# Cross-attention query products taken out of the tile loop: a stage of their own, four tiles wide, with the products kept in DRAM

## The chip, the cores and the metric

One core of a Trainium2 chip runs the whole kernel. The metric is the device time of one execution in microseconds (us). The engines are TensorE (PE in the profile, with its weight loads as PEld), VectorE (DVE), ScalarE (ACT), GpSimd (POOL) and SyncE (SP), which issues every data DMA. SBUF is the on-chip memory of the engines, PSUM the eight banks into which TensorE writes.

## The reference, cut to what matters

```python
x = x + xattn(layernorm(x), ctx_768)     # x: (64, 32, 512); ctx_768: (64, 257, 384)
x = x + attn(layernorm(x))               # self-attention with a position bias
x = x + ffn(layernorm(x))                # gated, fake-quantized

def xattn(h, c):                         # 16 heads of 64
    q, k, v = h @ Wq, c @ Wk, c @ Wv
    scores = einsum('bhsd,bhkd->bhsk', q, k) / 8
    return (softmax(scores) @ v) @ Wo + bo
```

The change is in `xattn` alone.

## The kernel before

The 2048 tokens (64 batches of 32) are 16 tiles of 128 tokens, so a tile holds four batches. The three layers are three stages, one after the other. In the first, `pe_cross_tile` walks the tiles in a hardware loop. It never forms k or v. For each head it multiplies q by Wk first ("QK", `pe_qk` L468), which gives the query products `qk` with 384 rows, and then by the transposed context ("CT", `pe_ctxT`). The values are formed in the same way: probabilities by context ("PV"), then by Wv ("WV") and by Wo ("WO").

Many products are made in float32 precision out of reduced-precision parts: an operand is split into a high part (ScalarE copies it with rounding, `act_split`) and a low part (VectorE subtracts, `dve_low` L695), and three products high*high, high*low and low*high are added up in PSUM. The scores S, PV and WO are made so. The query projection Q (L464, 128x128 operands) and QK (L475, 64 rows, two heads side by side in the two halves of the array) are plain float32 products, which stand in the profile as two instructions each.

TensorE's order in one tile is written out by hand: for each batch b the scores S(b, 0..3) of four groups of rows; between them the transposes PT and PL of the previous batch's probabilities, then its PV(0..2), and the transposes CT of the next batch's context. Batch 0 has no previous one in the tile: there the transposes XT of the next tile's normalized x and its projection Q(0), Q(1) stand. After batch 3 come QK for the next tile in six parts, with PT, PL and PV of batch 3 between them, then WV, then WO. VectorE, ScalarE and GpSimd have lists in the same order; each bank has three semaphores (filled, copied, drained) that count its uses. GpSimd splits the context rows (`pool_split`, L863 high, L866 low). VectorE's list holds the layernorm of the tile after next (19 small dependent steps and two wide ones), the row maxima (L799), the reciprocals (L774) and scaling of probabilities (L777), all low parts, and `oT` (L791). SyncE's list holds the loads of context (L887), x and the stores of the result.

Of the kernel before, what the change touches and what calls it, by code (L numbers as in the profile page):

```python
# [6 lines left out]
ALU = mybir.AluOpType  # L7
# [29 lines left out]
def cross_units(last):  # L37

    u = []

    def pT(b):
        return [(("PT", b, 0), "t1"), (("PT", b, 1), "t0"), (("PL", b), "t1")]

    def pv(b, m):
        return [(("PV", b, m), ("o0", "o1")[(b * 3 + m + 1) % 2])]

    def qk(i):
        banks = (("s0", "s1"), ("q0", "q1"))[i % 2]
        return [(("QK", i // 3, i % 3, par), banks[par]) for par in range(2)] if not last else []

    def ct(b, c):
        return [(("CT", b + 1, c), ("t0", "t1")[c % 2])] if not (last and b == 3) else []

    def q(n):
        return [(("Q", n), ("q0", "q1")[n])] if not last else []

    for b in range(4):
        before = b > 0
        u.append((("S", b, 0), "s0"))
        u += pT(b - 1)[0:2] if before else []  # L60
        u.append((("S", b, 1), "s1"))
        if not last and b == 0:
            u.append((("XT",), "o0"))
        u.append((("S", b, 2), "s0"))
        u += pT(b - 1)[2:3] if before else []
        u.append((("S", b, 3), "s1"))
        u += pv(b - 1, 0) if before else []
        u += ct(b, 0) + ct(b, 1)
        u += pv(b - 1, 1) if before else q(0)
        u += ct(b, 2)  # L70
        u += pv(b - 1, 2) if before else q(1)
    u += qk(0) + pT(3)[0:2] + qk(1) + pT(3)[2:3] + qk(2) + pv(3, 0) + qk(3) + pv(3, 1) + qk(4) + pv(3, 2) + qk(5)
    u += [(("W", 0), "t0"), (("W", 1), "t1"), (("WO",), "o1")]
    return u
# [61 lines left out]
def build_kernel(nc, x, ctx_768, Wq, Wk, Wv, Wo, bo, a_Wq, a_Wk, a_Wv, a_Wo, rel_emb, clip_x, clip_down,  # L136
# [22 lines left out]
    with ctx:  # L159
# [10 lines left out]

# [6 lines left out]
        x_ln = sb("x_ln", [P, D], F32)  # L177
        x_res = sb("x_res", [P, D], F32)
        x_nrm = sb("x_nrm", [P, D], F32)
# [8 lines left out]
        wq = sb("wq", [P, KD, INNER], F32)  # L188
        qk = sb("qk", [P, 2, 4, KC, 4, P], F32R)
        wkT = sb("wkT", [P, KI, DC], F32)  # L190
        xnT = sb("xnT", [P, KD, P], F32)
        p_last = sb("p_last", [P, 512], F32)
        qT = sb("qT", [P, KI, P], F32)

        aT_low = nc.alloc_sbuf_tensor_at("aT_low", [P, KI, P], F32R, offset=sb.where["xnT"])
        aT_high = nc.alloc_sbuf_tensor_at("aT_high", [P, KI, P], F32R, offset=sb.where["qT"])
# [4 lines left out]
        bo_all = sb("bo_all", [P, D], F32)  # L201
        oT = sb("oT", [P, KC, HEADS, 4, SQ], F32)
        wk_raw = nc.alloc_sbuf_tensor_at("wk_raw", [P, KC, INNER], F32, offset=sb.at - KC * HEADS * P * 4)
        c_raw = sb("c_raw", [P, 2, DC], F32)
        c_nat = [sb(f"c_nat{i}", [P, 2, 2, DC], F32R) for i in range(2)]
        cT = [sb(f"cT{i}", [P, 2, KC, SKP], F32R) for i in range(2)]
        probs = [sb(f"probs{i}", [P, 4, SKP], F32) for i in range(2)]
        pT = sb("pT", [P, 2, 2, 512], F32R)
        c_last = sb("c_last", [P, 2, KC], F32)

        rem_rows = nc.alloc_sbuf_tensor_at("rem_rows", [NB, DC], F32, offset=sb.where["probs0"])
        remT = sb("remT", [P, 2, KC, NB], F32R)
        nmax = sb("nmax", [P, 4], F32)
        den = sb("den", [P, 4], F32)
        rden = sb("rden", [P, 4], F32)

# [75 lines left out]
        s_wq = sem("wq_loaded")  # L292
        s_wvo = sem("wv_wo_bo_loaded")
        s_xln = sem("x_ln_loaded")
        s_xres = sem("x_res_loaded")
# [1411 lines left out]
```

## Time and profile before

| | before |
|---|---|
| median of 3 runs | 1826.18 us (1825.54 to 1827.83) |
| span of the profiled execution | 1826.2 us |
| one tile in the steady loop | 70.05 us |
| last WO of cross-attention begins | 1162.24 us |
| TensorE busy over the span | 95% |

The profile's page gives nothing around the span: the times are those of the span, and the span of the profiled execution stands 0.0 us from the median. How to read it: busy shares of TensorE are of a pipelined engine, so the distance from one group's start to the next group's start says what a group really takes; VectorE and ScalarE times can be taken as they stand.

### The profile page before, as it was taken

The page shows a single profiled execution, that of the slowest core. Times are in us where ns is not written, and L with a number is a line of the kernel's source. Part 1 is how long each engine was busy: PE and PEld are TensorE (multiplying, and loading weights), DVE is VectorE, ACT ScalarE, POOL GpSimd, SP SyncE. Part 2 cuts the span into 40 slices and gives each one's busy share as a digit, 9 for nine tenths or more (in the row PEclk, how much of TensorE's full clock was granted, in tenths as well). Part 3 has the DMA queues.
Part 4 walks back from the last instruction along what each step waited for, and adds up shares of the span by engine and source line. Part 5 has one row for each costly group of instructions (what it writes and reads, how often), then busy time and mean ns, then how long its engine had stood idle before and what let it go on. Part 6 is the DMA issues. An engine that isn't in the chain of part 4 may idle for free.

```text
span 1826.2 us, 41682 instructions
## 1 busy us (share of the span) xinstructions
PE 1732.6 (95%) x15355; PEld 1486.9 (81%) x15367; DVE 1242.4 (68%) x3118; ACT 676.8 (37%) x1471; POOL 309.9 (17%) x183
## 2 busy tenths in 40 slices
PE   6899999999999999999999999899999999996778
PEld 6788988988988988988889888798989898973333
DVE  4767667667677676676676676477868686656686
ACT  3334334334334334334344443322222222213556
POOL 3312212122122122112122121100000000000334
PEclk8999999999999999999999999999999999997899
DMA  5110110110101101001101002501110101003002
GB/s 204 33 35 26 35 43 26 34 39 30 34 29 40 34 29 34 32 30 39 34 26 43 29 26 82 185 29 46 40 57 30 57 29 36 17 23 114 32 16 92
DMA packets 45218, 84.46 MB, mean 46 GB/s; under 512 B 3904, under 2 KB 20352, under 8 KB 45184
## 3 DMA queue, kind: packets, MB, share of 16 engines
q1 hardware_dynamic: 45184, 84.01, 14.0%
q8 instruction: 21, 0.34, 0.1%
q14 instruction: 13, 0.11, 0.0%
HBM read 71.41 MB, written 12.58 MB: 46 GB/s over the span
## 4 chain that ended last, share of the span: by engine, by line
PE 54%; issue 32%; DVE 8%; ACT 4%; POOL 1%; DMA 1%; DVEq 0%; SPq 0%; ACTq 0%; POOLq 0%
PE psum_o L537 15%; PE psum_s L505 10%; PE psum_q L464 6%; PE psum_t L551 5%; PE psum_o L563 5%; PE psum_s L475 3%; PE psum_t L485 3%; PE psum_q L475 2%; PE psum_o L1209 2%; PE psum_s L1209 2%; DVE nmax L799 2%; DVE oT L791 1%; DVE qk L695 1%; PE psum_t L523 1%; ACT probs L652 1%
## 5 line engine op out<-in xcount | busy, mean ns | idle before, releaser
L505 PE MATMUL psum_s<-cT,qk 128*128 128x258 f32 x2304 | 319.1, 289 | 10.7 <-ACT probs L652 7.5
L537 PE MATMUL psum_o<-pT,c_nat 128*128 128x512 f32 x1152 | 312.4, 407 | 0.0
L505 PEld LDWEIGHTS psum_s<-cT,qk 128*128 128x128 f32 x2304 | 292.9, 191 | 23.6 <-ACT probs L652 15.2
L863 POOL TENSOR_TENSOR c_nat<-c_raw,zero 128x768 fp32r<-128x768 f32 x64 | 93.9, 1467 | 870.6 <-PE psum_o L537 521.3
L652 ACT ACTIVATE probs<-psum_s,nmax 128x257 f32<-128x257 f32 x256 | 122.0, 476 | 312.7 <-DVE nmax L799 312.7
L537 PEld LDWEIGHTS psum_o<-pT,c_nat 128*128 128x128 f32 x1152 | 202.5, 188 | 41.4 <-DVE oT L791 0.3
L791 DVE SCALAR_TENSOR_TENSOR oT<-p_last,c_last,psum_o 128x512 f32<-128x512 f32 x192 | 142.8, 744 | 44.2 <-PE psum_o L537 30.6
L799 DVE TENSOR_REDUCE nmax<-psum_s 128x1 f32<-128x257 f32 x256 | 107.3, 419 | 88.6 <-PE psum_s L505 86.4
L695 DVE TENSOR_TENSOR pT<-psum_t,pT 128x512 fp32r<-128x512 f32 x128 | 86.3, 685 | 54.1 <-ACT pT L633 54.1
L464 PE MATMUL psum_q<-xnT,wq 128*128 128x128 f32 x1024 | 123.0, 280 | 0.0
L464 PEld LDWEIGHTS psum_q<-xnT,wq 128*128 128x128 f32 x1024 | 120.5, 197 | 0.0
L866 POOL TENSOR_TENSOR c_nat<-c_raw,c_nat 128x768 fp32r<-128x768 f32 x64 | 119.7, 1870 | 5.0
L931 PEld LDWEIGHTS psum_o<-xnT,w2q 128*128 128x128 f32 x1024 | 118.3, 194 | 2.2 <-issue 1.0
L931 PE MATMUL psum_o<-xnT,w2q 128*128 128x128 f32 x1024 | 118.6, 277 | 0.8 <-issue 0.8
L931 PE MATMUL psum_q<-xnT,w2k 128*128 128x128 f32 x1024 | 117.0, 275 | 0.0
L931 PEld LDWEIGHTS psum_q<-xnT,w2k 128*128 128x128 f32 x1024 | 115.6, 192 | 0.0
L777 DVE TENSOR_SCALAR probs<-probs,rden 128x257 f32<-128x257 f32 x256 | 107.9, 421 | 9.0
L633 ACT ACTIVATE cT<-psum_t 128x256 fp32r<-128x256 f32 x192 | 66.7, 382 | 95.5 <-PE psum_t L485 95.4
L695 DVE TENSOR_TENSOR cT<-psum_t,cT 128x256 fp32r<-128x256 f32 x192 | 75.3, 420 | 34.6 <-ACT cT L633 34.6
L551 PE MATMUL psum_t<-oT,wv 128*64 128x128 f32 x1536 | 87.4, 274 | 1.0 <-DVE oT L791 1.0
L551 PEld LDWEIGHTS psum_t<-oT,wv 128*64 128x64 f32 x1536 | 83.5, 137 | 4.0 <-DVE oT L791 4.0
L1010 PE MATMUL psum_t<-w2o_high,aT 128*128 128x512 f32 x256 | 83.4, 397 | 2.2 <-DVE aT L1112 2.2
(180 smaller groups left out, 2878.1 us busy)
## 6 DMA issues: line engine op xcount, KB each, us to landing
c_raw<-in_ctx_dram SPq DMA_DIRECT2D x64, 384.0 KB, 3.2
out_dram<-x_out SPq DMA_DIRECT2D x32, 256.0 KB, 2.0
x_ln<-in_x_dram SPq DMA_DIRECT2D x16, 256.0 KB, 2.7
x_res<-in_x_dram SPq DMA_DIRECT2D x16, 256.0 KB, 3.2
x_ln<-out_dram SPq DMA_DIRECT2D x16, 256.0 KB, 2.8
x_res<-out_dram SPq DMA_DIRECT2D x16, 256.0 KB, 2.9
x_all<-out_dram SPq DMA_DIRECT2D x1, 4096.0 KB, 15.7
out_dram<-o_sb SPq DMA_DIRECT2D x16, 256.0 KB, 2.0
```

The lines of the kernel that those rows point to most:

```text
L464: i = pe.matmul(ps[:, j * P:(j + 1) * P], wq[:, k, (4 * n + j) * P:(4 * n + j + 1) * P], xnT[:, k, :], start=k == 0, stop=k == KD - 1)
L505: i = pe.matmul(ps[:, 0:SKP], qk[:, part, rg, c, b, :], cT[b % 2][:, moving, c, :], start=n == 0, stop=n == 3 * KC - 1)
L537: i = pe.matmul(ps[:], c_nat[b % 2][:, part, k, cols], pT[:, moving, k, :], start=n == 0, stop=n == 5)
L551: i = pe.matmul(ps[64 * par:64 * par + 64, h4 * P:(h4 + 1) * P], wv[:, c, head * DH:(head + 1) * DH], oT[:, c, slot, :, :], start=c == 0, ...
L652: nc.scalar.activation(probs[b % 2][:, rg, 0:SK], bank[bk][:, 0:SK], ACT.Exp, bias=nmax[:, rg:rg + 1], accum_out=den[:, rg:rg + 1]).then_i ...
L695: nc.vector.tensor_tensor(out, in_(bank[b]), high.bitcast(F32), ALU.subtract).then_inc(drained[b], 1)
L777: nc.vector.tensor_scalar(probs[b % 2][:, rg, 0:SK], probs[b % 2][:, rg, 0:SK], rden[:, rg:rg + 1], None, ALU.mult).then_inc(s_dve, 1)
L791: nc.vector.scalar_tensor_tensor(oT[:, m, :, b, :], p_last[:].rearrange("p (s q) -> p s q", q=SQ), c_last[:, b % 2, m:m + 1], bank[bk][:]. ...
L799: nc.vector.tensor_reduce(nmax[:, rg:rg + 1], bank[bk][:, 0:SK], AX_X, ALU.max, negate=True).then_inc(s_max, 1)
L863: G.tensor_tensor(c_nat[i][:, 0, :, :].rearrange("p k n -> p (k n)"), c_raw[:].rearrange("p k n -> p (k n)"), zero[:].to_broadcast([P, 2 * ...
L866: G.tensor_tensor(c_nat[i][:, 1, :, :], c_raw[:], c_nat[i][:, 0, :, :].bitcast(F32), ALU.subtract).then_inc(s_pool, 1)
L931: i = pe.matmul(ps[:, j * P:(j + 1) * P], w[:, k, (4 * n + j) * P:(4 * n + j + 1) * P], xnT2[:, k, :], start=k == 0, stop=k == KD - 1)
```

## The change

1. A stage before the loop makes Q and QK for all 16 tiles, in four groups s of four tiles. Its operands are split into parts: Wq (`wq`, 2 parts), x (`xnT`), Wk (`wkT`) and q (`qT`); a matmul is now 512 tokens wide. The order in a group is Q(0..3), QK(0..3), Q(4..7), XT of the next group, QK(4..7).
2. QK is copied as whole float32 numbers into `staged`, four slots (j modulo 4), by ScalarE (even heads) and VectorE (odd heads), and stored in `qk_dram`, 3 MiB per tile, 48 MiB in all; each store writes runs of 1536 bytes. A slot is written again only after its store has landed (`wait_slot`).
3. In the loop, one tile's products are loaded back into `raw` (3 MiB), and split in SBUF into `qk`: four high copies of 128x1536 on ScalarE (`act_qk_high`), four subtractions of 128x1536 on VectorE (`dve_qk_low`), both in the loop's batch 3 for the next tile.
4. The loop has no XT, Q, QK and layernorm. Every batch now is the same step: S, PT, PL, PV of the batch before (also across the tile border), CT. WV of the tile before stands in batch 1, WO of it in batch 3; after the last tile a tail does batch 3's PT, PL and PV, then WV and WO.
5. The scaling of probabilities is shared: groups 0 and 1 on ScalarE, 2 and 3 on VectorE. The last key's copies go to ScalarE. Scores use three banks (s0, s1, q0, s0) instead of two. The context has two raw buffers. The split of Wo goes from GpSimd to ScalarE and VectorE, in the first tile; Wv, Wo and x are loaded after the last store of the stage has landed.

```diff
-            for i in range(6):
-                if not last:
-                    pe_qk(pe, t, i // 3, i % 3)
...
+        def pe_group_q(pe, s, j):
...
+            for k in range(KD):
+                for part, moving in PARTS:
+                    m = pe.matmul(ps[:], wq[:, part, k, j * P:(j + 1) * P], xnT[:, moving, k, :, :],
+                                  start=(k, part, moving) == (0, 0, 0), stop=(k, part) == (KD - 1, 1))
...
+        def pe_group_qk(pe, s, j):
...
+            for c in range(KC):
+                places = [empty(pe, project(("QK", s, j, c, par))) for par in range(2)]
+                for part, moving in PARTS:
+                    for par in range(2):
+                        r = slice(64 * par, 64 * par + 64)
+                        m = pe.matmul(places[par][0][:], wkT[r, part, j, c * P:(c + 1) * P], qT[r, moving, j, :, :],
+                                      start=(part, moving) == (0, 0), stop=part == 1)
...
+        def pe_cross_tile(pe, t, section):
+            begun, more = section != "first", section != "last"
             for b in range(4):
+                before = begun or b > 0
+                pe_scores(pe, t, b, 0, section)
+                if before:
+                    pe_probsT(pe, t, b, section)
+                pe_scores(pe, t, b, 1, section)
+                if b == 1 and begun:
+                    pe_wv(pe, t, 0, section)
+                pe_scores(pe, t, b, 2, section)
+                if before:
+                    pe_probs_last(pe, t, b, section)
+                if b == 1 and begun:
+                    pe_wv(pe, t, 1, section)
+                pe_scores(pe, t, b, 3, section)
+                if before:
+                    pe_pv(pe, t, b, 0, section)
+                if more or b < 3:
+                    pe_ctxT(pe, t, b, section, (0, 1))
+                if before:
+                    pe_pv(pe, t, b, 1, section)
+                if b == 3 and begun:
+                    pe_wo(pe, t, section)
+                if more or b < 3:
+                    pe_ctxT(pe, t, b, section, (2,))
+                if before:
+                    pe_pv(pe, t, b, 2, section)
...
+        def act_qk_high(act, t, rg):
+            act.wait_ge(s_qraw, 16 * t + 16)
+            nc.scalar.activation(qk[:, 0, rg, :, :, :].rearrange("p c b (h q) -> p h (c b) q", h=4),
+                                 raw[:, rg, :, :].rearrange("p h (a q) -> p h a q", q=SQ), ACT.Copy).then_inc(s_qhi, 1)
...
+        def dve_cross_tile(dve, t, section):
...
             for b in range(4):
+                before, after = begun or b > 0, more or b < 3
+                qk_next = b == 3 and more
...
+                row_max(b, 3)
+                inverse(b, 2)
+                if qk_next:
+                    dve_qk_low(dve, t + 1, 0, section)
+                if before:
+                    dve_attended(dve, t, b, 0, section)
+                inverse(b, 3)
+                if qk_next:
+                    dve_qk_low(dve, t + 1, 1, section)
+                if after:
+                    ctxT(b, 0)
+                    ctxT(b, 1)
+                norm(b, 2)
                 norm(b, 3)
+                if before:
+                    dve_attended(dve, t, b, 1, section)
+                if b == 3 and begun:
+                    dve_x_out(dve, t, section)
+                if after:
+                    ctxT(b, 2)
+                if qk_next:
+                    dve_qk_low(dve, t + 1, 2, section)
+                if before:
+                    dve_attended(dve, t, b, 2, section)
+                if qk_next:
+                    dve_qk_low(dve, t + 1, 3, section)
...
+        def sp_project_all(sp):
...
+            load_ctx(sp, 0, 0)
+            load_ctx(sp, 0, 1)
+            for s in range(GROUPS):
+                if s < GROUPS - 1:
+                    sp.wait_ge(s_xp, GROUP * (s + 1))
+                    load_x_group(sp, s + 1)
+                if s == 2:
...
+                    load_qk(sp, 0, 0)
+                for j in range(8):
...
+                    for par in range(2):
+                        sp.dma_start(qk_dram[GROUP * s:GROUP * (s + 1), :, 2 * (j // 4) + par, j % 4, :].rearrange("t p n -> p t n"),
+                                     staged[:, j % 4, par, :, :]).then_inc(s_staged[j % 4], 16)
+            for i in range(4):
+                sp.wait_ge(s_staged[i], 64 * GROUPS)
+            sp.dma_start(wv[:], Wv.rearrange("(k p) n -> p k n", p=P)).then_inc(s_wvo, 16)
+            sp.dma_start(wo_raw[:], Wo.rearrange("(k p) n -> p k n", p=P)).then_inc(s_wvo, 16)
```

GpSimd's split for batch b of a tile still waits for the last PV of the batch before (`full(pool, U1(("PV", b - 1, 2), ...))`), and in the loop's batch 0 for the last PV of the tile before.

## Rows read from the trace of the kernel before

**Rows 1.** The page: busy time of each engine, share of the span, instructions.
```profile
PE 1732.6 (95%) x15355; PEld 1486.9 (81%) x15367; DVE 1242.4 (68%) x3118; ACT 676.8 (37%) x1471; POOL 309.9 (17%) x183
```

**Rows 2.** Windows of one loop step: us, busy us per engine (instructions), clock, DMA.
```profile
539.00:609.05 70.05, 69.07 (x573) 60.96 (x572) 47.83 (x124) 28.43 (x73) 14.63 (x9) 1.00 0.11 34
```

**Rows 3.** Timeline of TensorE, one tile: start, us, line, count, idle before it.
```profile
541.15 0.60 PE L449 MATMUL psum_o<-ident,x_nrm 128*128 128x128 f32 x4
541.51 2.40 PE L505 MATMUL psum_s<-cT,qk 128*128 128x258 f32 x18
...
544.18 3.74 PE L464 MATMUL psum_q<-xnT,wq 128*128 128x128 f32 x32
...
547.97 3.74 PE L464 MATMUL psum_q<-xnT,wq 128*128 128x128 f32 x32
...
551.47 1.34 PE L505 MATMUL psum_s<-cT,qk 128*128 128x258 f32 x9
...
552.64 1.04 PE L516 MATMUL psum_t<-ident,probs 128*128 128x128 f32 x8
...
553.44 2.40 PE L505 MATMUL psum_s<-cT,qk 128*128 128x258 f32 x18
...
555.68 0.60 PE L523 MATMUL psum_t<-ident,probs 128*128 128x128 f32 x4
...
557.25 1.56 PE L537 MATMUL psum_o<-pT,c_nat 128*128 128x512 f32 x6
...
558.64 0.60 PE L485 MATMUL psum_t<-ident,c_raw 128*128 128x128 f32 x4
...
562.28 1.24 PE L505 MATMUL psum_s<-cT,qk 128*128 128x258 f32 x9
```

**Rows 4.** The same timeline, the end of the same tile.
```profile
584.55 1.16 PE L475 MATMUL psum_s<-qT,wkT 64*128 64x128 f32 x16
585.64 1.09 PE L516 MATMUL psum_t<-ident,probs 128*128 128x128 f32 x8
...
598.09 5.46 PE L551 MATMUL psum_t<-oT,wv 128*64 128x128 f32 x96
603.48 0.50 PE L563 MATMUL psum_o<-wo_high,aT_high 128*128 128x512 f32 x1
...
609.05 2.31 PE L505 MATMUL psum_s<-cT,qk 128*128 128x258 f32 x18
```

**Rows 5.** Timeline of TensorE at the end of cross-attention.
```profile
1143.37 1.04 PE L516 MATMUL psum_t<-ident,probs 128*128 128x128 f32 x8
...
1162.24 0.39 PE L563 MATMUL psum_o<-wo_high,aT_low 128*128 128x512 f32 x1
```

**Rows 6.** Timeline of the start: the first layernorm on VectorE.
```profile
8.54 0.69 DVE L737 BATCH_NORM_STATS2 stats<-x_ln 128x6 f32<-128x512 f32 x1 [6.56 <-DMA x_ln<-in_x_dram]
...
12.84 0.55 DVE L747 TENSOR_SCALAR x_nrm<-x_ln,lnw 128x512 f32<-128x512 f32 x1
```

**Rows 7.** Groups of instructions by line and shape: busy us, mean ns; idle before.
```profile
L695 DVE TENSOR_TENSOR pT<-psum_t,pT 128x512 fp32r<-128x512 f32 x102 | 68.8, 685 | 43.7 <-ACT pT L633 43.7
L633 ACT ACTIVATE pT<-psum_t 128x512 fp32r<-128x512 f32 x102 | 55.1, 598 | 0.0
L1165 DVE TENSOR_TENSOR w2v_low<-w2v_raw,w2v_high 128x2048 fp32r<-128x2048 f32 x2 | 4.5, 2290 | 1.2 <-ACT w2v_high L1047 1.2
L1320 ACT ACTIVATE h_all<-h_all,tiny 128x1536 f32<-128x1536 f32 x8 | 12.5, 1563 | 0.0
```

**Rows 8.** Windows of stretches with loads of 4 KB rows, then one with stores.
```profile
1144.00:1154.00 10.00, 7.98 (x72) 6.39 (x72) 3.84 (x6) 1.68 (x3) 2.72 (x2) 1.00 1.03 410
...
1822.00:1823.00 1.00, 0.00 (x0) 0.00 (x0) 0.40 (x1) 0.00 (x0) 0.53 (x1) 1.00 0.70 262
```

**Rows 9.** Window around one load of context rows (1536-byte runs).
```profile
567.00:570.00 3.00, 2.78 (x17) 2.42 (x18) 2.50 (x11) 1.80 (x7) 0.00 (x0) 1.00 0.44 131
```

**Rows 10.** Timeline of GpSimd's splits and VectorE beside them.
```profile
503.64 1.47 POOL L863 TENSOR_TENSOR c_nat<-c_raw,zero 128x768 fp32r<-128x768 f32 x1 [7.70 <-PE psum_o L537]
...
504.41 0.72 DVE L713 TENSOR_TENSOR c_last<-remT 128x3 f32 x1
...
541.95 1.99 POOL L866 TENSOR_TENSOR c_nat<-c_raw,c_nat 128x768 fp32r<-128x768 f32 x1
...
543.39 0.70 DVE L777 TENSOR_SCALAR probs<-probs,rden 128x257 f32<-128x257 f32 x1
...
549.20 0.15 DVE L713 TENSOR_TENSOR c_last<-remT 128x3 f32 x1
...
564.15 1.85 POOL L866 TENSOR_TENSOR c_nat<-c_raw,c_nat 128x768 fp32r<-128x768 f32 x1
```

More of the change, by code:

```diff
@@ L539, in pe_pv @@
-            i.then_inc(filled[bk], 1)
-        def pe_wv(pe, t, n, last):
+                    taken(pe, U1(("PT", b, k), t, section))
+                pe.wait_ge(s_nat, 4 * t + b)
+            ps, done = empty(pe, U1(("PV", b, m), t, section))
+            for k in range(2):
+                for part, moving in PARTS:
+                    i = pe.matmul(ps[:], c_nat[(b - 1) % 2][:, part, k, m * P:(m + 1) * P], pT[:, moving, k, :],
+                                  start=(k, part, moving) == (0, 0, 0), stop=(k, part) == (1, 1))
@@ L660, in act_cross_tile, with ctxT @@
+            def ctxT(b, c):
+                act_high(act, U1(("CT", b, c), t, section), cT[(b + 1) % 2][:, 0, c, 0:2 * P], cols(2 * P))
             for b in range(4):
+                before, after = begun or b > 0, more or b < 3
                 exp(b, 0)
-                if b:
-                    act_probsT(act, t, b - 1, last)
+                if before:
+                    for k in range(2):
+                        act_probsT(act, t, b, k, section)
+                if b == 3 and more:
+                    act_qk_high(act, t + 1, 0)
@@ L702, in dve_last_key @@
[L702 to L714 removed]
+                scale(b, 1)
@@ new lines, in act_cross_tile, with act_cross_tail @@
+                act_last_scalars(act, b, 4 * t)
+                if after:
+                    ctxT(b, 2)
+                if b == 3 and more:
+                    act_qk_high(act, t + 1, 2)
+                    act_qk_high(act, t + 1, 3)
+                if section == "first" and b in (1, 2):
+                    act_wo_high(act, b - 1)
+        def act_cross_tail(act):
+            t, section = TILES, "tail"
+            for k in range(2):
+                act_probsT(act, t, 0, k, section)
+            act_probs_last(act, t, 0, section)
+            for n in range(2):
+                act_wv(act, t, n, section)
@@ L874, in pool_cross_tile, with dve_group_stats @@
[L874 to L880 removed]
+        GROUP_STEPS = 22
+        def dve_group_stats(dve, s):
+            ch = Chain(dve, GROUP_STEPS * s, s_lnp)
+            dve.wait_ge(s_xin, 16 * s + 16)
+            for i in range(GROUP):
+                ch.step(nc.vector.bn_stats(group_stats[:, i, :], x_in[:, i, :]))
+            dve.wait_ge(s_lnp, GROUP_STEPS * s + GROUP)
@@ new lines, in sp_cross_tile @@
+        def sp_cross_tile(sp, t, section):
+            begun, more = section != "first", section != "last"
+            for b in range(4):
+                if more or b < 2:
+                    sp.wait_ge(s_nat, 4 * t + (b + 1))
+                    load_ctx(sp, 4 * t, b + 2)
+                if b == 0:
+                    sp.wait_ge(s_qlo, 4 * t + 4)
+                    if more:
+                        load_qk(sp, t, 1)
+                    else:
+                        load_w2(sp, "q")
+            if not more:
+                taken(sp, U1(("S", 3, 3), t, section))
+                for name in "kvo":
+                    load_w2(sp, name)
+            if begun:
+                sp_x1(sp, t, section)
+                sp.dma_start(x_res[:], rows(x_rows, t)).then_inc(s_xres, 16)
```

1064 lines of the change are left out of this document (581 added, 483 removed).

## The prediction

> **What bounds the kernel now.** I began with the page's busy times [rows 1]: TensorE is busy for 95% of the span and the next engine, VectorE, for 68%. A share over the whole span says little about one stage, so I took the windows of one loop step next [rows 2]: of 70.05 us TensorE is busy for 69.07, VectorE for 47.8, ScalarE for 28.4, at full granted clock. The loop is bound by TensorE's own work; its waits are small. What each piece costs is read from the distance between starts in TensorE's timeline [rows 3, 4], since the busy times of overlapping matmuls are too long. The end of the stage is the last WO, 1162.24 + 0.39 = 1162.6 us [rows 5]. What follows (self-attention and FFN, 663.6 us) isn't changed, so the forecast is 663.6 plus the new time of cross-attention.
>
> **What the loop step loses.** Q(0) runs from 544.18 to the last CT at about 547.76 and Q(1) from 547.97 to 551.47, 7.1 us together; XT takes 0.36 [rows 3]. One QK part takes 585.64 - 584.55 = 1.09 us, six take 6.5 [rows 4]. So about 14 us of TensorE per tile go. The loop step that is left, from starts: four S at 1.12 (a pair takes 555.68 - 553.44 = 2.24) is 4.48; PT 0.80; PL about 0.39; three PV at 558.64 - 557.25 = 1.39 are 4.17; CT 0.36 and 0.19 is 0.55: 10.39 us per batch, against 562.28 - 551.47 = 10.81 measured for a batch now [rows 3]. I take 10.39, because the 0.4 of waits is for a score bank (three banks instead of two) and for the low part of CT (which VectorE reaches sooner, having two scalings less ahead of it). With WV 603.48 - 598.09 = 5.39 and WO 609.05 - 603.48 = 5.57 [rows 4], a step is 4 x 10.39 + 10.96 = 52.5 us if nobody waits.
>
> **Do the others keep up?** VectorE loses 12 low parts of QK (12 x 0.685 = 8.2) and gains four of 1536 elements with both inputs in SBUF: nearest row is 2.29 us for 2048 elements, so 4 x 1.75 = 7.0 [rows 7]. The layernorm (12.84 + 0.55 - 8.54 = 4.85 [rows 6]) and half of the scalings (about 3) go too: 47.8 becomes some 37 of 52.5. ScalarE loses 12 x 0.60 and the copies of q, and gains four copies of 1536 at 1.56 [rows 7], eight scalings and eight small copies: about 31 us. Neither is the bound. Loads per step are 3.1 MB more: 8 us of the DMA engines at 400 GB/s [rows 8], hidden under 52 us.
>
> **The tile border.** This is what I expect to cost. In batch 3 ScalarE gets to `qk_high` 2 and 3 only after the third CT, which stands behind WO. Counted from the end of S(3,3): CT(2) ends at 8.8, PV(3,2) at 10.2; ScalarE's `qk_high` 2 and 3 run 9.2 to 12.3; VectorE does `qk_low` 2 from 10.8 to 12.5, attended to 13.3, `qk_low` 3 to 15.0, and only then the first row maximum of the next tile. TensorE would want S(0,3) at 14.9, but it needs the exponential of S(0,0), which shares the bank: 15.0 + 0.4 + 0.5, about 1.1 late. PV(0,0) then waits 1.4 more for the low parts of PT, queued behind on VectorE: 2.5 us per border with no collision. GpSimd's split starts at PV(3,2)'s end, just there. The trace shows such a collision: a three-element addition of two SBUF inputs takes 0.72 and ends with GpSimd's instruction, 0.15 when nothing runs beside it; a scaling takes 0.70; and GpSimd's own low split takes 1.99 beside VectorE, 1.85 otherwise [rows 10]. If each `qk_low` queues with one split of 1.5 to 1.85, `qk_low` 3 ends at 16.9: 4.4 us per border. I take 3.7, nearer to the collision, since both start in the same microsecond. Step: 56.2 us.
>
> On that I weigh the Trainium skill, SBUF — State Buffer, section "Who interferes with whom": a VectorE instruction with two SBUF inputs and a GpSimd instruction that reads SBUF exclude each other for the whole instruction, and the one that comes first has the port. By that page the upper end, 4.4, is the sum for a border, and the time 10 us longer; the row of 1.99 shows far less than a whole instruction lost on GpSimd's side.
>
> **The stage in front.** TensorE per half group (four j): a 512-column matmul in parts takes 5.57/24 = 0.23 us (WO [rows 4]). Q is 12 of them per j, 2.75, four are 11.0. QK is 18 per j in pairs on the two halves of the array. Is a pair as dear as one? Now, 16 instructions of QK take 1.09, 68 ns each, where Q's take 3.5/32 = 110 ns [rows 3, 4]: a pair costs 1.24 of one, not 2. At 512 columns the weight load is a smaller part of each, so I take a pair at 0.24, near one: 9 x 0.24 = 2.15 per j, four are 8.6; at 1.24 they are 10.3, without overlap 16.5. XT is half of 16 transposes, 1. That is 20.6; copies run at 0.60 and 0.69 per bank [rows 7] against 0.7 per pair of banks, so bursts are just covered; I add 0.9 for XT banks and the layernorm steps between: 21.5. DMA per half group: 6.29 MB. Stores run at 262/0.70 = 374 GB/s [rows 8], a load of the same 1536-byte runs at 131/0.44 = 298 with its latency [rows 9]: 16.8 to 21.1 us, plus 1.3 for x. So stores hide, barely, and 21.5 holds. Start: 4 x 0.69 of statistics from 5.2 us, the chain of 3.6 [rows 6], four normalizations, a split of Wq's half (2.3), four low parts: first Q at 19; Q(0..3) 11, Wk's transposes and splits 5, first clock-limited stretch 2: first QK at 37. Stage: 37 + 7 x 21.5 + 9 = 196.5, and 6.5 for the early load of 3.1 MB among the stores and for slot waits: 203 us.
>
> **First tile and tail.** SyncE queues Wv, Wo, bo and x, and behind them the third context load, behind the wait for the last store. Stores end about 12 us after TensorE's last QK, 4.6 MB at 410 GB/s and landing take 14: the third context is there at 27, where TensorE wants it at 17. Tile 0 is 10.5 + 31.2 + 10 + the border, 56 us. Tile 15 has no next products, 52.5. The tail is today's last PT to last WO, 1162.6 - 1143.4 = 19.3 [rows 5].
>
> **Sum.** 203 + 56 + 14 x 56.2 + 52.5 + 19.3 = 1117.6, 45.0 less than 1162.6. The profiled span equals the median within 0.1 us, so 1826.2 - 45 = 1781 us.
>
> **Rivals.**
> 1. *The border costs nothing* (0.12): VectorE's queue recovers within S and PT; a step is 53.0, 14 x 3.2 = 45 less: 1736. For it: VectorE has 15 us free per step. Against it: the order puts two subtractions ahead of the first maximum.
> 2. *Stores are slow* (0.10). Place: `wait_slot`; every store scatters 1536-byte runs over DRAM rows 24 KB apart. At 200 GB/s a half group is 31.5 + 1.3 = 32.8 and the last store ends near 302, the third context comes at 316 instead of 230: +86, 1867, slower. It decides from 241 GB/s down (27.4 us a half group). For it: no row shows such a store in bulk; against it: 374 GB/s for 2 KB runs.
> The Trainium skill, DMA: Bandwidth & Descriptors, "Latency and other measured facts", gives 207 GB/s for a per-partition row pitch of 512 KiB and lets it fall with large powers of two; our pitch isn't a power of two, so the page gives this rival its plausibility and no more. No row here shows a pitch effect.
> 3. *Pairs of QK don't overlap at 512 columns* (0.08): a half group is 29.3, the stage 260, tile 0 waits 6 less: 1832, slower or the same. Against it: 68 ns beside 110.
> 4. *The even step waits in every batch* (0.10): the chain maximum, exponential, PT, high part, low part, PV no longer hides, 0.8 us more per batch, 60 batches: 1829.
> My forecast's own case has 0.60, and 1762 to 1802 as its own range (stage 192 to 215, border 2.5 to 4.4).
>
> **Range and chances.** The high end takes in rivals 3 and 4 in part, the low end part of rival 1: 1746 to 1829. The bound of a measurable change is 0.2%, 3.7 us. Faster: 0.60 + 0.12, half of rival 4 and some of 2 and 3: 0.80. Same 0.05. Slower 0.15, mostly rival 2.
>
> **What the profile will show.** Right: TensorE's start-to-start step near 56 with idle before S(0,3) and PV(0,0) named after VectorE; QK bursts of 8.6 us; DMA share near 0.8 to 1 through the stage; end of stage near 203; a wait for context in tile 0. Wrong: DMA at share 1 with under 300 GB/s and ScalarE or VectorE waiting for `qk_dram` (rival 2), QK of one j near 4.1 (rival 3), idle in each batch (rival 4). What would make me wrong most of all is the multiplier: one microsecond in the step is 15 in the end.

## The result, and the profile after

The changed kernel takes 1852.45 us (median of 4 runs, 1852.04 to 1855.51), against 1826.3 us before in the same session: a ratio of 1.0148, 95% interval 1.0134 to 1.0163. The forecast was 1781 us, with a range up to 1829. The change makes the kernel slower, by 26 us.

The page of the profiled execution (span 1853.7 us), its rows of busy time and of the granted clock; they answer to [rows 1]:

```profile
PE 1693.4 (91%) x13767; PEld 1443.9 (78%) x13767; DVE 1207.7 (65%) x2675; ACT 780.8 (42%) x1699; POOL 315.7 (17%) x179
...
PEclk9998988999999999999999999999999999997899
```

TensorE is busy for 39 us less than before, and the span has grown by some 27 all the same. Where it went is read from windows. First one step of the loop in each of its two forms (the columns of [rows 2], which these rows answer; the first from a tile's first S to the next tile's, the second from WO to WO), then single microseconds inside the first one:

```profile
516.38:574.50 58.12, 55.37 (x409) 49.42 (x408) 37.76 (x79) 29.19 (x79) 15.90 (x9) 0.97 0.26 90
...
627.04:687.50 60.46, 56.77 (x410) 50.27 (x408) 38.06 (x80) 29.33 (x79) 15.89 (x9) 0.94 0.25 87
...
524.00:525.00 1.00, 0.91 (x4) 0.91 (x5) 0.44 (x1) 1.00 (x3) 0.00 (x0) 0.50 1.59 415
525.00:526.00 1.00, 1.00 (x7) 1.00 (x6) 1.00 (x3) 0.40 (x3) 0.00 (x0) 0.50 0.32 98
```

A step was to last 56.2 us. From first WO matmul to first WO matmul thirteen of them last 58.1 to 60.5, on average (1105.38 - 334.46) / 13 = 59.3. Two things show: some 3 us in which TensorE does nothing, and a granted clock under 1.00. The clock is lost in one place, behind the tile border, where it is 0.50 (1.2 GHz) for three microseconds in this step, and for the whole of 644 to 650 in a later one. Over the fourteen borders of this trace behind the first the fall comes 7.4 to 10.1 us behind the tile's first S, and it lasts some 3 us at eight of them and 6 to 7 us at six.

The border in the timeline of TensorE (start, us, line, count, idle before it; it answers to [rows 3]):

```profile
516.38 1.24 PE L583 MATMUL psum_s<-cT,qk 128*128 128x258 f32 x9
517.46 1.03 PE L594 MATMUL psum_t<-ident,probs 128*128 128x128 f32 x8
518.25 1.32 PE L583 MATMUL psum_s<-cT,qk 128*128 128x258 f32 x9
519.93 1.34 PE L583 MATMUL psum_q<-cT,qk 128*128 128x258 f32 x9 [0.36 <-DVE qk L987]
521.11 0.60 PE L601 MATMUL psum_q<-ident,probs 128*128 128x128 f32 x4
524.10 2.30 PE L583 MATMUL psum_s<-cT,qk 128*128 128x258 f32 x9 [2.39 <-ACT probs L796]
526.38 2.06 PE L614 MATMUL psum_o<-pT,c_nat 128*128 128x512 f32 x6
```

The four groups of L583 are S(0,0) to S(0,3). The last begins 7.72 us after the first. In the later step the same two places look like this:

```profile
641.84 1.34 PE L583 MATMUL psum_s<-cT,qk 128*128 128x258 f32 x9 [2.39 <-ACT probs L796]
644.12 2.92 PE L614 MATMUL psum_o<-pT,c_nat 128*128 128x512 f32 x6 [0.94 <-issue]
```

Here S(0,3) still runs at full clock, and a third wait is seen, 0.94 us ahead of PV(0,0); in the first step S(0,3) at half clock covers it.

Back to the first step. S(0,3) waited for ScalarE's exponential of S(0,0), and that for VectorE, whose rows say why (the same stretch, VectorE and GpSimd, answering to [rows 10]):

```profile
516.72 1.47 POOL L1152 TENSOR_TENSOR c_nat<-c_raw,zero 128x768 fp32r<-128x768 f32 x1 [12.58 <-PE psum_o L614]
516.98 2.82 DVE L987 TENSOR_TENSOR qk<-raw,qk 128x1536 fp32r<-128x1536 f32 x1 [0.95 <-ACT qk L730]
...
518.26 3.23 POOL L1155 TENSOR_TENSOR c_nat<-c_raw,c_nat 128x768 fp32r<-128x768 f32 x1
519.72 0.73 DVE L1047 SCALAR_TENSOR_TENSOR oT<-p_last,c_last,psum_o 128x512 f32<-128x512 f32 x1
...
520.38 2.73 DVE L987 TENSOR_TENSOR qk<-raw,qk 128x1536 fp32r<-128x1536 f32 x1
...
523.03 0.41 DVE L1063 TENSOR_REDUCE nmax<-psum_s 128x1 f32<-128x257 f32 x1
```

`qk_low` 2 and 3 (L987) take 2.82 and 2.73 us where the same instruction takes 1.75 alone, and GpSimd's low split 3.23 instead of 1.85 [rows 10]. Each ends about one free duration after the other engine's instruction did: the first at 518.19 + 1.6, the split at 519.80 + 1.7, the second at 521.49 + 1.6. Only then comes the first row maximum, at 523.03.

The stage in front, in the timeline: SyncE ahead of group 1, VectorE and TensorE where that group's x is wanted, then TensorE's second such gap, the first S of the loop, the wait for the third context load in tile 0 and one for the third CT there:

```profile
64.38 11.06 SPq L1209 DMA_DIRECT2D qk_by_tile<-staged  x8
75.49 2.32 SPq L1177 DMA_DIRECT2D x_in<-in_x_dram  x1
...
88.34 2.47 DVE L916 BATCH_NORM_STATS2 group_stats<-x_in 128x6 f32<-128x512 f32 x4 [8.85 <-DMA x_in<-in_x_dram]
...
92.28 1.65 PE L511 MATMUL psum_q<-qT,wkT 64*128 64x512 f32 x6 [9.14 <-DVE staged L966]
...
145.87 1.65 PE L511 MATMUL psum_q<-qT,wkT 64*128 64x512 f32 x6 [9.33 <-DVE staged L966]
...
220.47 0.59 PE L583 MATMUL psum_s<-cT,qk 128*128 128x258 f32 x3 [1.86 <-DVE qk L987]
...
248.13 1.11 PE L554 MATMUL psum_t<-ident,c_raw 128*128 128x128 f32 x4 [8.71 <-DMA c_raw<-in_ctx_dram]
...
278.34 0.69 PE L554 MATMUL psum_t<-ident,c_raw 128*128 128x128 f32 x2 [2.91 <-DVE cT L856]
```

TensorE's row names `staged` L966, VectorE's copies of QK. These were not slow: they stood in VectorE's queue behind `group_stats`, which waited 8.85 us for x. SyncE issued that load only at 75.49, when all sixteen stores of the group before were issued (the row shows the last eight). It takes 12.8 us to land.

Windows in the stage (same columns): a half group without a wait, the half group with the first gap, and a stretch in which the DMA engines do nothing but stores.

```profile
113.80:134.20 20.40, 20.11 (x123) 16.62 (x122) 11.95 (x19) 9.92 (x17) 0.00 (x0) 1.00 0.77 269
...
80.80:113.80 33.00, 23.86 (x137) 19.78 (x136) 18.28 (x44) 11.19 (x20) 0.00 (x0) 0.84 0.70 244
...
44.00:60.00 16.00, 16.00 (x94) 13.24 (x91) 11.25 (x34) 6.75 (x13) 0.00 (x0) 1.00 1.03 365
```

The end of cross-attention, answering to [rows 5], is 1192.39 + 0.39 = 1192.8:

```profile
1192.39 0.39 PE L642 MATMUL psum_q<-wo_high,aT_low 128*128 128x512 f32 x1
```

So this part takes 30.2 us longer than before. What follows it takes 660.9, 2.7 less; no run looks into why.

### The profile page after: what moved, and what is told of

The parts are those of the page before. It is cut to its first block, busy times and chain, and to the rows that moved or that the text cites. A ratio compares the mean times of both kernels' runs of the same rounds, so it can differ in the third digit from the quotient of the medians.

```text
span 1853.7 us, 38185 instructions
## 1 busy us (share of the span) xinstructions
PE 1693.4 (91%) x13767; PEld 1443.9 (78%) x13767; DVE 1207.7 (65%) x2675; ACT 780.8 (42%) x1699; POOL 315.7 (17%) x179
## 4 chain that ended last, share of the span: by engine, by line
PE 53%; issue 31%; DVE 8%; ACT 3%; DMA 3%; SPq 1%; POOL 1%; DVEq 0%; ACTq 0%; POOLq 0%
PE psum_o L614 15%; PE psum_s L583 10%; PE psum_o L629 5%; PE psum_q L642 5%; PE psum_o L495 4%; PE psum_q L583 3%; PE psum_t L554 2%; DVE qk L987 2%; PE psum_t L594 2%; PE psum_o L1545 2%; DMA x_in<-in_x_dram 2%; PE psum_s L1545 2%; ACT qk L730 1%; PE psum_q L511 1%; PE psum_q L601 1%
## 5 line engine op out<-in xcount | busy, mean ns | idle before, releaser
L583 PE MATMUL psum_s<-cT,qk 128*128 128x258 f32 x1728 | 256.7, 294 | 42.4 <-ACT probs L796 38.4
L583 PEld LDWEIGHTS psum_s<-cT,qk 128*128 128x128 f32 x1728 | 229.5, 194 | 55.7 <-ACT probs L796 39.0
L1152 POOL TENSOR_TENSOR c_nat<-c_raw,zero 128x768 fp32r<-128x768 f32 x64 | 94.9, 1483 | 899.2 <-PE psum_o L614 672.3
L796 ACT ACTIVATE probs<-psum_s,nmax 128x257 f32<-128x257 f32 x192 | 91.8, 478 | 250.4 <-DVE nmax L1063 250.3
L987 DVE TENSOR_TENSOR qk<-raw,qk 128x1536 fp32r<-128x1536 f32 x64 | 141.0, 2205 | 15.9 <-ACT qk L730 15.6
L495 PE MATMUL psum_o<-xnT,wq 128*128 128x512 f32 x384 | 93.0, 402 | 4.9 <-DVE xnT L856 2.6
L730 ACT ACTIVATE qk<-raw 128x1536 fp32r<-128x1536 f32 x64 | 93.7, 1493 | 0.0
L495 PEld LDWEIGHTS psum_o<-xnT,wq 128*128 128x128 f32 x384 | 73.6, 194 | 23.4 <-issue 4.4
L629 PE MATMUL psum_o<-oT,wv 128*64 128x128 f32 x1536 | 90.7, 275 | 1.0 <-DVE oT L1047 1.0
L629 PEld LDWEIGHTS psum_o<-oT,wv 128*64 128x64 f32 x1536 | 83.2, 137 | 6.1 <-issue 4.0
L583 PE MATMUL psum_q<-cT,qk 128*128 128x258 f32 x576 | 82.7, 288 | 4.9 <-DVE qk L987 4.9
```

Of the source, the lines that this page charges most:

```text
L495: m = pe.matmul(ps[:], wq[:, part, k, j * P:(j + 1) * P], xnT[:, moving, k, :, :], start=(k, part, moving) == (0, 0, 0), stop=(k, part) == ...
L583: m = pe.matmul(ps[:, 0:SKP], qk[:, part, rg, c, b, :], cT[b % 2][:, moving, c, :], start=(c, part, moving) == (0, 0, 0), stop=(c, part) = ...
L629: i = pe.matmul(ps[64 * par:64 * par + 64, h4 * P:(h4 + 1) * P], wv[:, c, head * DH:(head + 1) * DH], oT[:, c, slot, :, :], start=c == 0, ...
L730: nc.scalar.activation(qk[:, 0, rg, :, :, :].rearrange("p c b (h q) -> p h (c b) q", h=4), raw[:, rg, :, :].rearrange("p h (a q) -> p h a ...
L796: nc.scalar.activation(probs[b % 2][:, rg, 0:SK], bank[bk][:, 0:SK], ACT.Exp, bias=nmax[:, rg:rg + 1], accum_out=den[:, rg:rg + 1]).then_i ...
L987: nc.vector.tensor_tensor(part[1], raw[:, rg, :, :].rearrange("p h (a q) -> p h a q", q=SQ), part[0].bitcast(F32), ALU.subtract).then_inc( ...
```

## The experiments

Every kernel was timed beside the kernel before on one chip (1828.74, 1827.94 and 1827.13 us in the three sessions), and has one profiled execution. "Step" is from first WO matmul to first WO matmul.

| kernel | median us | ratio to before, 95% | step us | clock in a step |
|---|---|---|---|---|
| changed | 1852.45 | 1.0148 (1.0134 to 1.0163) | 58.1 to 60.5 | 0.94 to 0.97 |
| changed, once more | 1854.46 | 1.0153 (1.0140 to 1.0167) | 59.2 to 60.5 | |
| x earlier | 1830.92 | 1.0018 (1.0009 to 1.0028) | 58.1 to 60.5 | |
| split later | 1802.64 | 0.9855 (0.9838 to 0.9871) | 55.7, three of 57.1 to 57.2 | 1.00, in the three 0.97 |
| third CT early, both lists | 1771.66 | 0.9688 (0.9671 to 0.9705) | 53.55 | 1.00 |
| filler behind the wait | 1839.62 | 1.0060 (1.0043 to 1.0077) | 58.63 | 1.00 |
| filler ahead of the wait | 1825.88 | 0.9988 (0.9979 to 0.9997) | 57.59 | 1.00 |
| third context load first | 1858.53 | 1.0158 (1.0142 to 1.0175) | 58.1 to 60.4 | |
| all four edits | 1744.83 | 0.9543 (0.9530 to 0.9556) | 53.55 | 1.00 |
| all but the later split | 1747.17 | 0.9561 (0.9548 to 0.9574) | 53.54 | |
| third CT early, TensorE only | 1802.51 | 0.9865 (0.9849 to 0.9880) | 55.48, the first 57.04 | 1.00, in the first 0.97 |
| VectorE's order only | 1861.58 | 1.0190 (1.0176 to 1.0204) | 58.8 to 61.1 | |

**x half a group earlier.**

```diff
-                if s < GROUPS - 1:
-                    sp.wait_ge(s_xp, GROUP * (s + 1))
-                    load_x_group(sp, s + 1)
+                if s == 0:
+                    sp.wait_ge(s_xp, GROUP)
+                    load_x_group(sp, 1)
...
                 for j in range(8):
+                    if j == 4 and s + 2 < GROUPS:
+                        sp.wait_ge(s_xp, GROUP * (s + 2))
+                        load_x_group(sp, s + 2)
```

> The x rows of group s+2 are loaded in the middle of group s, ahead of four stores, instead of behind the eight stores of group s. Theory A (order of the DMA queue): in the changed kernel VectorE's statistics wait 8.85 and 9 us for x_in, and TensorE stands 9.1 and 9.3 us in groups 1 and 2; both gaps go, the stage ends near 200 instead of 218.5 and the whole is 18 us shorter, about 1834. Rival B (bandwidth of the stores): the stage moves 50 MB at 362 GB/s, the gaps only move to the slots of staged, and the time stays within 5 us of 1852.

Both gaps are gone. The loop's first S, in the timeline of this kernel:

```profile
195.56 0.59 PE L583 MATMUL psum_s<-cT,qk 128*128 128x258 f32 x3 [1.86 <-DVE qk L987]
```

That is 24.9 us earlier: 18.5 of idle time, some 5 of half clock behind it (92.28 to 97.4 and 145.87 to 152.1, from the distances of the starts), and one that I can't place. The span falls by 26.4, the median by 22 (1852.45 to 1830.92). The queue's order is the cause of the stage's loss, shown by mending it.

**GpSimd's split later.** In the loop's batch 0 it waits until S(0,3) is done, when VectorE has both low parts behind it.

```diff
-                pool.wait_ge(filled["o1"], U1.before("o1", t, section))
+                full(pool, U1(("S", 0, 3), t, section))
```

> GpSimd's split of the tile's first batch starts after S(0,3) instead of at the last PV of the tile before; nothing else moves. Theory C (GpSimd and VectorE shut each other out at the border): qk_low 2 and 3 take 1.76 us instead of 2.8 each, S(0,3) waits 0.4 instead of 2.4 us, TensorE's clock stays at 1.00, a step takes 53.5 to 54.5 instead of 59.3, and the whole comes to 1770 to 1785. Rival D (it is the order of VectorE's and ScalarE's lists alone): S(0,3) still waits over 2 us and the time stays within 10 us of 1852.

A window of a step of this kernel:

```profile
500.00:555.67 55.67, 53.75 (x410) 48.15 (x409) 35.77 (x81) 29.06 (x78) 14.49 (x9) 1.00 0.25 94
```

And TensorE's two waits at its border, at S(0,3) and PV(0,0), in the timeline:

```profile
510.22 1.34 PE L583 MATMUL psum_s<-cT,qk 128*128 128x258 f32 x9 [0.98 <-ACT probs L796]
...
512.50 1.66 PE L614 MATMUL psum_o<-pT,c_nat 128*128 128x512 f32 x6 [0.94 <-issue]
```

L987's mean duration falls from 2205 to 1752 ns, and the time by 50 us. That is less than theory C gave and far from D's nothing: the collision is about half of the matter. What is left at the border is the order's part. The clock is back at 1.00 in eleven of the fourteen steps; in the other three it still falls for some 3 us, with the same two waits ahead of it.

**The third CT halfway through WO, on both lists.** TensorE puts CT(3,2) between WO's two halves, so `qk_high` 2 and 3 begin 2.8 us earlier; VectorE takes `qk_low` 2 ahead of `x_out` and `qk_low` 3 ahead of the attended sum.

```diff
             for k in range(KI):
+                if k == KI // 2:
+                    halfway()
...
-                    pe_wo(pe, t, section)
-                if more or b < 3:
+                    if more:
+                        pe_wo(pe, t, section, lambda: pe_ctxT(pe, t, b, section, (2,)))
...
-                if b == 3 and begun:
-                    dve_x_out(dve, t, section)
                 if after:
                     ctxT(b, 2)
                 if qk_next:
                     dve_qk_low(dve, t + 1, 2, section)
-                if before:
-                    dve_attended(dve, t, b, 2, section)
+                if b == 3 and begun:
+                    dve_x_out(dve, t, section)
                 if qk_next:
                     dve_qk_low(dve, t + 1, 3, section)
+                if before:
+                    dve_attended(dve, t, b, 2, section)
```

> In batch 3 the third CT stands in the middle of WO instead of behind it, and VectorE does both late qk_low ahead of its third oT. Theory D (order of the lists): ScalarE's last two high copies start 2.5 us earlier, the first row maximum of the next tile is 3 to 4 us earlier, no wait at S(0,3), step 53 to 54.5, whole 1765 to 1785. Rival C (the shared port alone sets it): the collision with GpSimd stays, S(0,3) waits 1.5 us or more, gain under 30 us.

A window of a step of this kernel:

```profile
500.00:553.55 53.55, 53.53 (x410) 48.13 (x409) 35.72 (x80) 29.10 (x78) 15.90 (x10) 1.00 0.27 98
```

There is no idle time and no lost clock: TensorE's own work is 53.55 us a step. The split stands where it stood, and the collision is still there, but now VectorE comes first and GpSimd pays for it (the same border in this kernel):

```profile
499.06 1.75 DVE L992 TENSOR_TENSOR qk<-raw,qk 128x1536 fp32r<-128x1536 f32 x1
...
499.28 2.85 POOL L1157 TENSOR_TENSOR c_nat<-c_raw,zero 128x768 fp32r<-128x768 f32 x1 [12.62 <-PE psum_o L614]
```

GpSimd's high split takes 2.85 us instead of 1.47 (1774 ns on average, 1483 in the changed kernel), and nobody waits for it. The 53.55 also splits the loss of the changed kernel: 59.3 - 53.55 = 5.75 us a step.

**Is part of it the clock?** Unneeded transposes into a free bank, ahead of S(0,3). The first kernel had 28 of them, in the lines of the diff below but two lines further down, behind the wait on `s_qlo`:

> TensorE does 28 spare transposes (about 2.5 us) into an empty bank just before S(0,3) of each tile but the first, whose results are overwritten. The queues of the other engines and the wait itself are as before. Theory E (the wait costs twice, because the granted clock falls to half behind it): the clock stays 1.00 in the loop, the step loses the 3.3 us that are not idle time and not work, 15 steps, whole about 1803 (1795 to 1815). Rival F (what is slow behind the border is slow for another reason, or the clock falls anyway): the time stays at 1850 or grows by up to 10.

The clock was full, but the step 58.63. The filler stood behind the wait for the fourth low part, not ahead of it, and began only when that wait ended (timeline of this kernel):

```profile
520.91 3.27 PE L581 MATMUL psum_o<-ident 128*128 128x128 f32 x28 [1.53 <-DVE qk L991]
523.94 1.33 PE L587 MATMUL psum_s<-cT,qk 128*128 128x258 f32 x9
```

S(0,3) came 9.89 us after S(0,0) (514.05), 2.2 later than without it, so the run measured two things at once. The second has 20 transposes and puts them ahead of that wait:

```diff
+            if b == 0 and rg == 3 and section != "first":
+                spare_bank, _ = empty(pe, U1(("PV", 0, 0), t, section))
+                for _ in range(20):
+                    pe.transpose(spare_bank[:, 0:P], ident[:], ident[:])
             if b == 0:
                 pe.wait_ge(s_qlo, 4 * t + (rg + 1))
```

> Clock theory: of the 3.1 us that a step lasts longer than the sum of the prediction, 2 to 3.5 us are not idle time but the half clock (1.2 GHz) behind the 2.4 us of idle time ahead of S(0,3). Twenty unneeded transposes (some 2.2 us), now ahead of the wait for the fourth low part, fill the gap without making it longer, where the first filler began only behind that wait and overshot by 2.2 us: S(0,3) begins 7.7 to 8.0 us after the tile's first S as in the changed kernel, the clock stays at 1.0, a step lasts 56.0 to 57.0 us, the whole 1805 to 1820 us. Rival (the wait itself is the whole loss, and the products behind it would wait for VectorE anyway): step 58.6 to 59.3, whole 1840 to 1853 us.

A window of a step of this kernel:

```profile
506.78:564.37 57.59, 56.18 (x430) 50.38 (x429) 37.80 (x80) 29.10 (x79) 15.87 (x9) 1.00 0.26 91
```

And its border in TensorE's timeline:

```profile
513.85 1.24 PE L587 MATMUL psum_s<-cT,qk 128*128 128x258 f32 x9
...
519.02 2.35 PE L579 MATMUL psum_o<-ident 128*128 128x128 f32 x20
...
521.57 1.34 PE L587 MATMUL psum_s<-cT,qk 128*128 128x258 f32 x9 [0.20 <-ACT probs L800]
...
523.76 1.64 PE L618 MATMUL psum_o<-pT,c_nat 128*128 128x512 f32 x6 [0.85 <-issue]
```

S(0,3) begins 7.72 us after S(0,0), exactly as without the filler, and every step is 57.59. So the half clock is 59.3 - 57.6 = 1.7 us of the step, less than the 2 to 3.5 that the clock theory had, and the waits are 57.59 - 53.55 = 4.04. Neither theory's range held the time; the truth lies between them, and the split of the loss is now measured. The 1.7 is net, and it goes with the trace: in the second trace of the changed kernel the thirteen steps are 59.8 on average, which makes it 2.2. Little of it is lost at S(0,3), since PV(0,0) would wait for the low part of PT all the same: it begins 2.19 us behind S(0,3) here and 2.28 in the changed kernel. It is lost in the PV and CT behind.

**The two halves of the border edit.** First TensorE's alone:

> Half of the border edit: only TensorE's third CT of batch 3 goes halfway through WO; VectorE's order stays, so it still takes x_out at WO's end first. Order theory: qk_low 2 then begins at WO's end + 0.2 + 0.69 + 0.42, some 0.9 us earlier than now, everything behind it in the step 0.9 earlier, the collision with GpSimd's split unchanged: 14 steps by 0.9, 12 to 15 us, and up to 20 more if the clock no longer falls: 1818 to 1842 us. Rival (the gain of the whole edit, 84 us, comes from the third CT alone): 1770 to 1785.

The gain is 52 us, not 12 to 35 and not the whole edit's 82. The 0.9 us is there (`qk_low` 2 begins 0.24 us ahead of S(0,0), 508.48 against 508.72, instead of 0.60 behind it), but I had the collision unchanged, and it isn't. VectorE and GpSimd in this kernel:

```profile
508.48 1.75 DVE L992 TENSOR_TENSOR qk<-raw,qk 128x1536 fp32r<-128x1536 f32 x1
...
509.06 2.49 POOL L1157 TENSOR_TENSOR c_nat<-c_raw,zero 128x768 fp32r<-128x768 f32 x1 [12.62 <-PE psum_o L614]
...
510.81 2.36 DVE L992 TENSOR_TENSOR qk<-raw,qk 128x1536 fp32r<-128x1536 f32 x1
```

VectorE now begins 0.6 us before GpSimd, and GpSimd pays: its high split takes 2.49 instead of 1.47. `qk_low` 3, behind that split, loses 0.6. Together VectorE loses 0.6 instead of 2.05 (1.07 + 0.98), and with the 0.9 that is 2.35 of the border's 4.04; the steps say 57.59 - 55.48 = 2.11. And the clock stays at 1.00 in thirteen of the fourteen steps (S(0,3) waits 0.73 to 0.82 us in all of them), which is the other 1.7.

Then VectorE's order alone:

> The other half: only VectorE's order is changed (x_out and the attended sum behind the two low parts of the third and fourth QK), the third CT stays behind WO. Order theory: x_out (0.69) loses the cover of the wait for the third CT and comes in line ahead of qk_low 3, while the attended sum (0.73) leaves it, so the first row maximum comes at about the same time: 1848 to 1860 us. Rival (the order on VectorE is what mattered): at least 30 us faster than the changed kernel, under 1823.

1861.6 against 1854.5 us for the changed kernel in that session, so 7 slower: just above the range of the order theory, and the rival is out. The wait at S(0,3) is 3.04 instead of 2.39, the 0.69 of `x_out`. Reordering VectorE is worth something only once the third CT is early: there it brings the remaining 1802.5 to 1771.7.

> The changed kernel itself, as it stands, beside the two halves on one chip, as their base line and to see how far its own time and its mix of steps of 58.1 and 60.4 us go from run to run: 1850 to 1858 us.

1854.46 us (1853.46 to 1858.30), and all fourteen steps were 59.2 to 60.5 in its trace, with none of the 58.1 to 58.4 of the first. The mix of steps changes from run to run, so a difference of a few microseconds against this kernel says little.

**The third context load ahead of Wv and Wo.**

```diff
+            sp.wait_ge(s_nat, 1)
+            load_ctx(sp, 0, 2)
             for i in range(4):
                 sp.wait_ge(s_staged[i], 64 * GROUPS)
...
-                if more or b < 2:
+                if (more or b < 2) and not (section == "first" and b == 0):
                     sp.wait_ge(s_nat, 4 * t + (b + 1))
                     load_ctx(sp, 4 * t, b + 2)
```

> Queue theory: TensorE's wait of 8.7 us for the third context half in tile 0 is SyncE's order (its load is issued behind the wait for the last stores and behind Wv and Wo). Issued ahead of them it lands before TensorE wants it: the wait goes, and some half clock with it, 1841 to 1846 us. Rival (the DMA engines are still busy with the stores, so the load lands no earlier, or Wv is late in its place): 1850 to 1854 us.

In the trace the wait of 8.7 us is gone, and one for the next context load takes its place (4.23 us, at 255.04); the first WO comes at 329.33 and the span is 1848.0. The first WO of the changed kernel comes at 334.46 in one trace and at 331.31 in the other, so that is 2 to 5 us. The five runs went from 1849.78 to 1858.64 us and show no gain; the queue theory's 1841 to 1846 is out, and the median lies above the rival's range too. Inconclusive by the time. The trace agrees with the rival's reason: the DMA engines are busy throughout from 240 to 250 us (share 1.07), so the loads are short of DMA time there and not only badly ordered.

**All four edits, and all but the later split.**

> The mended order with all four edits (x loads half a group earlier, third context load first, split of the context behind S(0,3), third CT halfway through WO with VectorE's qk_low 3 ahead of its scaling). If the losses are separate they add: 25 + 10 + 84 us off 1853.7 gives 1735 us (1728 to 1742). Rival (the mended stage and tile 0 only shift a wait to the next late thing, or the step is already at TensorE's own work so that the later split adds nothing but a new wait): 1742 to 1760 us.

> As the kernel with all four edits, but with GpSimd's split back at its old place. Slack theory: once VectorE has qk_low 2 and 3 done early, nothing waits for them, and the collision of the split with a qk_low costs VectorE up to 1.4 us that it has spare: within 3 us of the kernel with all four edits. Port theory (the collision stays on the path at the border): 0.5 to 1.5 us per step, 8 to 22 us slower than that kernel.

1744.83 and 1747.17 us: 4.6% and 4.4% below the kernel before. The span of the first is 110 us below the changed kernel's; the single edits' spans add up to 26 + 84 + 6 = 116 without the split. Most but not all adds up, and the time lies in the rival's range (1742 to 1760), not in the sum's. In the trace 3 to 5 us of idle time stay at tile 0's border, and 2.6 to 4.0 for the context load. The intervals of the two kernels overlap and their steps are equal, so the later split is worth nothing once VectorE is early: the slack theory's time is right and the port theory's is wrong, for this order. The reason is not quite the slack theory's: with the split at its old place it is GpSimd's high split that takes 2.85 us, and at the steady loop's borders `qk_low` takes 1.74 to 1.76.

## Why the prediction was wrong

The forecast for the end of cross-attention was 1117.6 us, measured 1192.8: 75 too little. Two steps failed. The border was priced as a wait and nothing more, 3.7 us at full clock, and it costs 5.75: 4.04 of waits and 1.7 of half clock behind them. And the x load of the stage was charged its 1.3 us of bandwidth, without its place in SyncE's queue, and it costs 24.9 in all. The terms, with each tile cut at its first S:

| term | forecast | measured | error |
|---|---|---|---|
| stage, to the end of its last QK | 203 | 218.6 | +15.6 |
| tile 0, without a border | 51.7 | 62.8 | +11.1 |
| tiles 1 to 14 | 786.8 (56.2 each) | 831.1 (59.4 each) | +44.3 |
| tile 15, with the border ahead of it | 56.8 | 59.4 | +2.6 |
| tail | 19.3 | 20.9 | +1.6 |

The prediction counts a border at the end of a tile, so that tile 0's 56 holds one and tile 15's 52.5 none; the wait is seen behind the next tile's first S, so here the one of tile 0 (4.3) stands with the tiles behind. The number of borders, fifteen, was right.

**What bounds the kernel** was right: TensorE's own work, and without waits it does shrink to 53.55 us a step, as the three kernels with the early CT show.

**The step's work** was forecast at 52.5: 1.05 short of 53.55. In the kernel with all four edits batches are 10.47 instead of 10.39, batch 0 10.76, and batch 1, where WV stands, 16.41: WV, now cut in two halves of 48 matmuls with scores between them, costs 16.41 - 10.47 = 5.94 us instead of the 5.39 of [rows 4].

**The border** is the first step that failed, by a missing term more than by its size. I worked out 2.5 us without the collision and 4.4 with it. The runs give 55.67 - 53.55 = 2.1 and 57.59 - 53.55 = 4.04. Both prices were near, and the difference between them, 1.9, was right. I took 3.7 between them, from the row of 1.99 in [rows 10]. That row was the wrong witness: beside that split VectorE ran only short instructions (0.15 to 0.70 us), so there was no long one for the split to wait for, as there is with a subtraction of 1.75 us. The Trainium skill, SBUF — State Buffer, section "Who interferes with whom", says that a VectorE instruction with two SBUF inputs and a GpSimd instruction that reads SBUF exclude each other for the whole instruction and that the first has the port. This case's trace agrees in both directions: 2.82 and 2.73 for 1.75 on VectorE, 3.23 for 1.85 on GpSimd, and 2.49 for 1.47 on GpSimd where VectorE came first. But the measured 4.04 is only 0.35 us above my price, 5 us in the end, a small part of the 75.

The missing term was **the clock**. The idle stretch of 2.4 us is followed by S, PV and CT at 1.2 GHz: 1.7 us per step on average, 24 us over 14 steps, more than the error of the waits. I had priced a wait at its own length. Per step the error of 3.1 is 1.05 of work, 0.35 of border and 1.7 of clock.

**Tile 15** lasts 52.7 us with the border mended (third CT early), 0.2 from my 52.5; the other 2.4 us of its error are the border's, 6.7 for my 4.3.

**The stage.** The first QK comes at 38.6 (37 forecast). The burst of QK is 8.9 us (8.6 forecast), so pairs overlap and rival 3 is false; a half group without a wait is 20.4, or 21.8 where XT stands in it (21.5 forecast); the stores run at 353 to 366 GB/s over stretches of 12 to 16 us, so rival 2 is false with its place and its price. The second step that failed is that I charged the x load its 1.3 us of bandwidth and did not ask where it stands in SyncE's queue. It is issued behind the last store of the group, and VectorE's copies of the banks stand behind its consumer: 9 us each time, twice, and half clock behind each. With the load mended the stage ends at 193.7. So my 203 had 9 us to spare, among them the 6.5 for slot waits and the early load, of which the mended stage shows no trace (no Q or QK behind its first one waits more than 0.23 us). That the stage is only 15.6 off is luck: two errors, 24.9 and 9.3, stand against each other.

**Tile 0** has the wait for the third context half where I put it, 8.71 us for my 10. What I didn't have is the third CT's low part (2.91, VectorE busy with the low parts), seven shorter waits (6.9 together), and half clock (granted 0.87 over 218 to 281). Against them, its first batch, which has no PT, PL and PV, takes less than the 10.5 that I gave it.

**The other rivals.** The border is not free (rival 1), though it could be made so: the kernels with the early CT are that case. No batch but the border's waits (rival 4): batch 2 lasts 10.47 us. My slower side was put down to slow stores, which were fast; it came by the border, which I named as the multiplier ("one microsecond in the step is 15 in the end") and did not give a case of its own with the clock in it. Both bounds of my own case were passed: the stage by 3.6 us (218.6 for 215) and the border by 1.35 (5.75 for 4.4). VectorE's "some 37" us per step should have been 38.75 by its own terms; it measured 37.8, and nothing hung on it.

**Open.** Why some steps have 3 us of half clock and others 6 to 7, with the same idle time ahead of them, isn't settled; nor why the clock falls at three borders of the kernel with the later split and at one with TensorE's edit alone, and not at their others, with the same waits of under 1 us; nor what tile 0 still loses when all edits are in.

## What to carry to other kernels

When a loop's order puts a long instruction of a helper engine between the last tile and the first product of the next, price the stall with the half clock behind it, times the number of tiles; here 4.0 and 1.7 us in a step. Then look whether the thing that is late can start earlier: two transposes moved half a WO forward, with VectorE's list changed to match, gave 82 us where taking away the collision gave 50. A load's bandwidth isn't its price: ask behind which stores it is issued and who stands behind its consumer.

Idle rows understate a stall. At the border the first step's rows name 0.36 + 2.39 = 2.75 us, because the half clock covers the third wait; with it they name 3.69, and the step lost 4.04 without the clock.

## What the hardware showed that was not expected

- TensorE's clock fell to half behind the gap of 2.4 to 3.0 us at every border of the kernels that have it, but not always at once: S(0,3), right behind the gap, took 1.9 to 2.3 us at five of the fourteen borders of the changed kernel and 1.34 to 1.53 at the others, where the PV behind it was slow. It stayed at full where transposes filled the gap, and with gaps of 0.7 to 1 us at most borders (13 of 14 and 11 of 14), though not at every one.
- A VectorE subtraction of 1536 elements with both inputs in SBUF and a GpSimd split take turns as whole instructions: 2.82 and 3.23 us where each alone takes 1.75 and 1.85. Which of the two begins first decides who pays: with VectorE 0.2 us ahead its subtraction took 1.75 and GpSimd's split 2.85 instead of 1.47.
- A store from SBUF to DRAM in runs of 1536 bytes across rows 24 KB apart ran at 353 to 366 GB/s over stretches of 12 to 16 us, as fast as the one microsecond of stores seen before ([rows 8], 262 GB/s at a DMA share of 0.70).
